# Grouped attention: one head's eight matmuls between the context products, statistics by tile, ScalarE's weights in two pieces

## The reference, cut to what matters

```python
q  = _ln(_fp8_linear_pertensor(ln_out, wq, ...))        # 8 groups x 2 heads of 128
k  = _ln(_fp8_linear_pertensor(ln_out, wk, ...))        # 8 groups x 128
v  = _fp8_linear_pertensor(ln_out, wv, ...)
core = _gqa(q, k, v)
qx = _ln(_fp8_linear_pertensor(ln_out, wqx, ...))       # 8 groups x 2 heads of 128
kx, vx = jnp.split(jnp.einsum('bsi,oi->bso', cond, w_kv_x), 2, axis=-1)
kx = _ln(kx)
xout = _gqa(qx, kx, vx)
catq = _div_clamp_fp8(jnp.concatenate([core, xout], -1), proj_smooth)
return jnp.einsum('bsi,oi->bso', catq, wproj) * (proj_in_scale * proj_w_scale)
```

## Time and profile before

| | |
|---|---|
| median of three runs | 2054.92 us (2054.7 to 2056.19) |
| the profiled execution's own time | 2054.24 us |
| its span, first to last instruction | 2052.5 us |
| mean granted TensorE clock | 0.993 |
| PE busy | 1987.3 us (97%) |
| PEld (weight loads) busy | 1568.8 us (76%) |
| DVE busy | 1406.6 us (69%) |
| ACT busy | 1229.2 us (60%) |
| POOL busy | 687.7 us (34%) |

### The profile page before, as it was taken

One profiled execution on the slowest core, in us unless ns is written; L12 is line 12 of the kernel. 1 busy time (PEld: TensorE's weight loads), 2 busy tenths in 40 slices (PEclk: granted clock), 3 DMA queues, 4 the chain that ended last, 5 costly groups with the idle time before them and its releaser, 6 DMA issues. The chain is left out here.

```text
span 2052.5 us, 31495 instructions
## 1 busy us (share of the span) xinstructions
PE 1987.3 (97%) x11048; PEld 1568.8 (76%) x11068; DVE 1406.6 (69%) x3154; ACT 1229.2 (60%) x3187; POOL 687.7 (34%) x689
## 2 busy tenths in 40 slices
PE   8999999999999999999998999999999999998998
PEld 5644789888988888898876886665766785666997
DVE  2397677777777776767567847676677658995555
ACT  2073687878887888788773445553544446772332
POOL 1300354454445454545330002324351102332442
PEclk9999999999999999999999999999999999999999
DMA  4033434232424242332323204313232220003200
GB/s 187 10 122 124 136 89 148 85 137 88 150 87 137 83 148 89 131 90 87 109 81 107 73 3 158 128 70 128 109 116 107 82 87 22 2 2 138 94 1 32
DMA packets 60173, 193.66 MB, mean 94 GB/s; under 512 B 9408, under 2 KB 28640, under 8 KB 56048
## 3 DMA queue, kind: packets, MB, share of 16 engines
q1 hardware_dynamic: 48496, 172.15, 24.5%
q10 hardware_dynamic: 9504, 8.50, 1.4%
q0 software_dynamic: 2016, 11.01, 1.3%
HBM read 171.75 MB, written 19.48 MB: 93 GB/s over the span
## 5 line engine op out<-in xcount | busy, mean ns | idle before, releaser
L988 PE MATMUL psum<-la_w_both,context 128*128 128x256 f32 (+1 forms) x1536 | 343.7, 380 | 0.0
L988 PEld LDWEIGHTS psum<-la_w_both,context 128*128 128x128 f32 (+1 forms) x1536 | 277.6, 184 | 44.9
L1465 POOL TENSOR_TENSOR norm_std<-room 128x400 f32<-128x400 f32 x75 | 70.4, 938 | 271.6 <-DVE room L1230 271.5
L944 PE MATMUL psum<-qa_xqf,qa_two 128*128 128x400 f32 x640 | 156.2, 372 | 2.3 <-PEq L60 2.3
L944 PEld LDWEIGHTS psum<-qa_xqf,qa_two 128*128 128x128 f32 x640 | 115.4, 191 | 7.5 <-issue 3.2
L3021 ACT ACTIVATE it_prob<-psum,it_nm 100x257 f32<-100x257 f32 (+1 forms) x256 | 101.7, 415 | 30.1 <-DVE it_nm L3048 29.3
L1458 POOL TENSOR_TENSOR room<-room,qa_inv 128x500 f32<-128x500 f32 x64 | 89.7, 1401 | 52.8 <-DMA qa_inv<-qa_std_rows 50.6
L1006 PE MATMUL psum<-qa_kxT,room 128*100 128x361 f32 x256 | 99.8, 471 | 3.9 <-ACT qa_kxT L1148 2.8
L1154 ACT ACTIVATE qa_prob<-psum,qa_nm 100x361 f32<-100x361 f32 x128 | 72.0, 562 | 47.3 <-DVE qa_nm L1319 46.7
L1154 ACT ACT_TABLE_LOAD x64 | 82.1, 1283 | 24.0 <-ACT qa_size L1172 18.2
L2574 POOL TENSOR_TENSOR gf_last_diff<-la_gf_what,la_gf_w 128x512 bf16<-128x512 bf16 x24 | 27.0, 1145 | 206.4 <-issue 170.2
(11 more groups left out here) (399 smaller groups left out, 5289.2 us busy)
## 6 DMA issues: line engine op xcount, KB each, us to landing
context<-in_context SPq DMA_DIRECT2D x70, 722.0 KB, 4.7
qa_inv<-qa_std_rows SPq DMA_DIRECT2D x64, 250.0 KB
qa_w_raw<-in_qa_w SPq DMA_DIRECT2D x8, 1536.0 KB, 16.1
la_gf_raw<-in_gf_w SPq DMA_DIRECT2D x16, 768.0 KB, 4.8
qa_piece<-in_tf_pieces ACTq DMA_DIRECT2D x64, 128.0 KB, 2.1
la_w_qt<-in_qa_o SPq DMA_DIRECT2D x8, 1024.0 KB, 6.1
gf_ternary<-la_gf_made POOLq DMA_DIRECT2D x7, 768.0 KB
gf_ternary<-keep POOLq DMA_DIRECT2D x7, 768.0 KB
```

What stands on the lines that cost most here:

```text
L944: mm = pe.matmul(psum[:, bank, 0:HALF], two[:, part, j, k, :], xqf[:, PART_XQ[j], k, (h % 2) * HALF:(h % 2 + 1) * HALF], start=(k == 0 and ...
L988: mm = pe.matmul(psum[0:rows, i // 2, (i % 2) * 256:(i % 2) * 256 + 256], ctxT[:, n % 2, k, t0:t0 + rows], kv_raw[:, s, k, :], start=(k == ...
```

## The change

Five things change, all inside `grouped_attention`.

1. The unit behind is no longer laid in two halves around the transposes of the probabilities. Its eight matmuls come one by one from a generator, one after each context chunk. The context product asks for one after each of its 12 chunks and there are eight, so four lie in the first tile, four in the second, and none in the third. This holds from step 6 on (`OUT_LAG`); in the steps before, the unit keeps its two halves as before.
2. `ctx_mm` counts 3 a step, one for each tile. VectorE takes the statistics of the first two tiles when the second is done, and those of the third when it is done.
3. VectorE's `normalise_keys(n)` comes ahead of `probs_out(n-1)`.
4. ScalarE's scaling of the weights (`scale_weights`) moves ahead of the exponentials; the writing of the high part stays behind them. An activation with Exp draws that table's load ahead of the scaling.
5. ScalarE takes the context values of the first two tiles from PSUM before it waits for the statistics, not after.

```diff
-                    sp.wait_ge(S_["ctx_mm"], n + 1)
+                    sp.wait_ge(S_["ctx_mm"], 3 * n + 3)
                     sp.dma_start(ctxT[:, n % 2], a["context"][(n + 2) % B]).then_inc(ctx_in[n % 2], 16)
...
-            def project_unit(u, chunks=range(C)):
+            def unit_products(u, chunks=range(C)):
                 h, j = half_and_part(u)
                 bank = bank_of(u)
...
                         mm = pe.matmul(psum[:, bank, 0:HALF], two[:, part, j, k, :],
                                        xqf[:, PART_XQ[j], k, (h % 2) * HALF:(h % 2 + 1) * HALF],
                                        start=(k == 0 and part == 0), stop=(k == C - 1 and part == 1))
-                if chunks[-1] == C - 1:
-                    mm.then_inc(S_["unit_mm"], 1)
+                        if k == C - 1 and part == 1:
+                            mm.then_inc(S_["unit_mm"], 1)
+                        yield
+
+            def project_unit(u, chunks=range(C)):
+                for _ in unit_products(u, chunks):
+                    pass
...
-            def project_context(g, s, b, n):
+            def project_context(g, s, b, n, beside):
...
                         mm = pe.matmul(psum[0:rows, i // 2, (i % 2) * 256:(i % 2) * 256 + 256],
                                        ctxT[:, n % 2, k, t0:t0 + rows], kv_raw[:, s, k, :],
                                        start=(k == 0), stop=(k == C - 1))
-                mm.then_inc(S_["ctx_mm"], 1)
+                        if k < C - 1:
+                            next(beside, None)
+                    mm.then_inc(S_["ctx_mm"], 1)
+                    next(beside, None)
...
-                project_context(g, s, b, n)
-                around = n
-                for u in behind(n):
-                    project_unit(u, range(C // 2) if around else range(C))
+                beside = unit_products(behind(n)[0]) if not early(n, OUT_LAG) and behind(n) else iter(())
+                project_context(g, s, b, n, beside)
+                if early(n, OUT_LAG):
+                    for u in behind(n):
+                        project_unit(u, range(C // 2) if n else range(C))
                 if not early(n, 1):
                     turn_probs(n - 1)
-                for u in behind(n) if around else ():
-                    project_unit(u, range(C // 2, C))
-                if not early(n, OUT_LAG):
+                if early(n, OUT_LAG):
+                    for u in behind(n) if n else ():
+                        project_unit(u, range(C // 2, C))
+                else:
                     project_out(*out_chunk(g, b, n))
...
                 measure(g, s, b, n)
+                if not early(n, 1):
+                    act.activation(spare[:, 1:2], core.eps[1.0], ACT.Exp)
+                scale_weights(n)
                 for u in ahead(n):
                     high_squares(u)
                 if not early(n, 1):
                     exps(n - 1)
                 high_weights(n)
                 if not early(n, 1):
-                    act.activation(spare[:, :], core.eps[1.0], ACT.Sqrt)
+                    act.activation(spare[:, 0:1], core.eps[1.0], ACT.Sqrt)
+                act.wait_ge(S_["ctx_st"], 3 * n + 2)
+                act.activation(vx[:, b % 2, 0:2, :], psum[:, 0, :].rearrange("p (i o) -> p i o", i=2)[:, :, P:2 * P],
+                               ACT.Copy)
                 act.wait_ge(S_["stats_ready"], n + 1)
                 act.activation(sd[:, :], mv[:, :, 1], ACT.Sqrt, bias=core.eps[1e-5]).then_inc(S_["sd_ready"], 1)
-                act.activation(vx[:, b % 2, 0:2, :], psum[:, 0, :].rearrange("p (i o) -> p i o", i=2)[:, :, P:2 * P],
-                               ACT.Copy)
                 act.activation(vx[0:R2, b % 2, 2, :], psum[0:R2, 1, P:2 * P], ACT.Copy)
...
             def context_stats(n):
-                dve.wait_ge(S_["ctx_mm"], n + 1)
                 for i, (_, rows) in enumerate(TILES):
+                    dve.wait_ge(S_["ctx_mm"], 3 * n + max(i, 1) + 1)
                     dve.bn_stats(st[0:rows, i, :], psum[0:rows, i // 2, (i % 2) * 256:(i % 2) * 256 + P]).then_inc(
                         S_["ctx_st"], 1)
...
                 context_stats(n)
+                normalise_keys(n)
                 if not early(n, 1):
                     probs_out(n - 1)
-                normalise_keys(n)
```

More of the change, by code:

```diff
@@ L798, in grouped_attention @@
         st, mv, sd, nmr = sb("st", [P, 3, 6]), sb("mv", [P, 3, 2]), sb("sd", [P, 3]), sb("nmr", [P, 3])
-        out_scale, spare = sb("out_scale", [P, 1]), sb("spare", [P, 1])
+        out_scale, spare = sb("out_scale", [P, 1]), sb("spare", [P, 2])
         nm, sums, rsum = sb("nm", [T, 4]), sb("sums", [T, 4]), sb("rsum", [T, 4])
@@ L890, in load @@
                 if g + 1 < G:
-                    sp.wait_ge(S_["ctx_mm"], max(1, g * B))
+                    sp.wait_ge(S_["ctx_mm"], 3 * max(1, g * B))
                     sp.dma_start(kv_raw[:, 1 - slot], a["qa_kv"][g + 1]).then_inc(S_["kv_in"], 16)
@@ L1119, in heads_out, with scale_weights @@
                 last.then_inc(S_["heads_ready"], 1)
-            def high_weights(n):
+            def scale_weights(n):
                 made = part_made(n, 1)
@@ L1131, in high_weights @@
                     last.then_inc(S_["v_scaled"], 1)
-                    act.wait_ge(S_["v_scaled"], g)
-                    act.activation(v3[:, g % 2, 0], w_raw[:, :, V_COL:V_COL + P], ACT.Copy).then_inc(S_["v_hi"], 1)
                     return
@@ L1140, in high_weights @@
                 last.then_inc(S_["w_scaled"], 1)
+            def high_weights(n):
+                made = part_made(n, 1)
+                if not made:
+                    return
+                g, j = made
+                if j == PARTS:
+                    act.wait_ge(S_["v_scaled"], g)
+                    act.activation(v3[:, g % 2, 0], w_raw[:, :, V_COL:V_COL + P], ACT.Copy).then_inc(S_["v_hi"], 1)
+                    return
+                u, own = (g - 1) * PARTS + j, slice(PART_COL[j], PART_COL[j] + P)
                 act.wait_ge(S_["w_scaled"], u + 1)
@@ L1219, in _ @@
                 nrm.root(act, 0, i)
-            act.activation(spare[:, :], core.eps[1.0], ACT.Gelu)
+            act.activation(spare[:, 0:1], core.eps[1.0], ACT.Gelu)
         @block.vector
```

## The result

The changed kernel takes 2081.72 us (median of four runs, 2079.31 to 2084.18) against 2055.49 (four runs of before, 2054.7 to 2056.19): a ratio of 1.0128, 95% interval 1.011 to 1.0145. It is slower, by 26.2 us. The profiled executions agree: the span went from 2052.5 to 2078.9 us, +26.4.

The account below looks back on a forecast made before the run. TensorE was taken as the bound, busy 700.74 of 701 us, so every new wait counts in full. 15.1 + 15.1 + 3.4 - 1.8 - 2.2 = +29.6 us gave 2084 us, own range 2074 to 2092, overall 2064 to 2098.

Parts of the forecast that it names:

- its own case: Whole kernel: the summed terms hold, +29.6 us, 2084 us, range 2074 to 2092; chance 0.61.
- 1 the alternation itself: TensorE, unit matmuls among context passes: taken as 0, bounds 5.9 us gained to 5 us lost.
- Part 3: Unit's first matmul waits for VectorE's low weights where n % 8 = 6: 2.16 us standstill, 7 times, 15.1 us.
- Part 2: Chains from the last context pass E: variance 0.34 us late at 39 boundaries, weighing 0.13 at 14; 15.1 us.
- Part 4: Clock falls to half after the pauses of about 2 us: 2 of 7, 3.4 us, bounds 0 and 11.9.
- Part 5: ScalarE's scaling before exponentials: their 0.5 us lateness is covered, cost 0; late variance where n % 8 = 6 goes, -1.8 us.
- 6 steps 59 to 62: End of the stage: shorter chain to the scores, E+4.64 instead of E+5.18; four boundaries by 0.54, -2.2 us.
- the case without cover: ScalarE's exponentials late with nothing covering them: 0.5 x 35 = 18 us.
- second reading: TensorE: alternation hides the weight load, 0.014 us off each of 424 matmuls, -5.9 us; rival total 2045, chance 0.05.

Follow-up runs that it names:

- low part early: Changed kernel, but where n % 8 = 6 VectorE makes the weights' low part ahead of the score maxima: 2062.7 us, ratio to before 1.0031.
- short square: Changed kernel with the low part made before the maxima where n % 8 = 6, and GpSimd squaring only half of each unit's columns: 2059.26 us, one run.
- edit 1 alone: Kernel before with only the unit's matmuls one by one between the context products, none of the other four edits: 2109.94 us, ratio 1.0263.
- two halves: Changed kernel with the unit's eight matmuls back in two halves around the probabilities' transposes, other edits kept: 2050.27 us, ratio to before 0.9971.
- probabilities first: Changed kernel with the low part made before the maxima where n % 8 = 6, and VectorE's probabilities again ahead of the keys: 2066.92 us, ratio 1.0051.
- eighth experiment: Changed kernel, low part before maxima (n % 8 = 6), probabilities before keys, GpSimd squaring and subtracting half the columns, ScalarE scaling one of three head tiles: 2043.81 us, one run.

## Why the prediction was right

It gave 2084 with 2074 to 2092 for its own case; 2081.7 was measured. By its own terms, against the profiled execution:

```
term                                      predicted   measured
1 the alternation itself                       0         0       0.614 a period against 0.614
2 late chains, boundaries to 7 to 59       +15.1     +14.8      (low part early: 13.1 + 7 x 0.25)
3 standstill at the weights                +15.1     +14.8      7 x 2.12
4 the clock                                 +3.4      +3.3      2 falls of 1.66
5 late variance, n % 8 = 6                  -1.8      -1.8
6 steps 59 to 62                            -2.2      -1.5
  steps 0 to 5                               0        -1.5
  outside the steps                          0        -1.5
```

**Part 3** was right in place, count and size: 2.16 forecast, 2.12 found, and removed by moving one instruction. Reading the code for which step makes a part and which step uses it gave it; nothing in the profile of before points to it, because there the part was ready at 732.58 and the unit started at 735.15, 2.6 us later.

**Part 2** was right in sum and partly right in kind. It put the squares last, 0.34 late, and the weighing at 0.13. The weighing was worth 0.21 to 0.24, which is what steps after an "ahead" unit lost and what the short square left, and the squares only what came on top: 0.28 us less on GpSimd brought 0.05. The start was near (0.16 late against 0.13), but the sum passed that lateness on as it was, and it grew to 0.23 by the key transposes. So the sum came out right partly by luck: 39 boundaries lost 0.29 instead of 0.34, and 14 lost 0.22 instead of 0.13. The other forecast times were near: variance E+4.67 against 4.63 (the hand-over on GpSimd took 0.08, 727.67 to 727.75, and not 0.14), copy of the keys E+4.97 against 4.89, root E+0.71 against 0.72. Three chains that end within 0.1 us of one another can't be ranked by such a sum, and it does not matter for the total, but it does for the mending: shortening one of them alone gained almost nothing, or moved the wait.

**Part 4** was a draw from few cases, and luck. Of the five pauses between 1.76 and 1.99 us in the trace of before three were followed by a fall, which would have given four of seven; I took two. Two is what the profiled execution had; the run with edit 1 alone had three falls behind the same pauses. The four runs of the changed kernel span 4.9 us, about three falls, and the slowest had the lowest granted clock (0.989 against 0.991 and 0.992). Not all of them need be these: behind step 62, where nothing was changed but the end of the stage, the profiled executions of the eleven kernels had three to seven falls.

**Part 5** held in the changed kernel: the transposes never waited. The run with two halves shows the cover was needed: with the unit behind the context product again, the early scaling costs 0.35 us in the steps with n % 8 = 3. It is 6 x 0.35 = 2.1 us there, and not the 0.5 x 35 = 18 us that I had put on the case without cover: in the other steps the late exponentials were still in time.

**Left out or too small.** I set steps 2 to 5 at zero, and they gave 1.9 us back, step 0 another 0.4, as the unit keeps its old place there and only the shorter chain shows. Step 1 took 0.8 us more (16.94 against 16.13): TensorE stands there for 2.93 us instead of 1.88, and both kernels have a fall of the clock there. This step is between 14.6 and 17.0 us in the eleven kernels, and no run isolates why.

In steps 59 to 62 I expected 0.54 a boundary and found 0.15, 0.30, 0.30 and 0.77 (the last in step 62, where in the kernel before the transposes of the probabilities start at E+0.63 and in the changed one at E-0.16). The chain ends at the copy of the keys at E+4.77, not 4.54. TensorE, held at the weighing, hands over the transposed keys later. TensorE and ScalarE in step 61 of the changed kernel, where E is 1075.01:

```profile
1078.62 0.48 PE L1006 MATMUL psum<-ident,qa_nrm_x 128*128 128x128 f32 x3
1079.13 0.65 ACT L1169 ACTIVATE qa_kxT<-psum,params 128x361 f32<-128x361 f32 x1 [0.21 <-PE psum L1006]
```

ScalarE stands idle for 0.21 us until the transposes are done. With the probabilities first the weighing is on time, the transposes start at E+3.38 instead of 3.61, and the copy ends at E+4.70 although the normalised keys come later. So the term took the squares out of the ScalarE chain and forgot the chain over TensorE beside it.

The 1.5 us outside the steps stay unexplained. Over the eleven kernels the time before step 0 is 206.7 to 207.8 us and that from step 63 on 984.8 to 989.1, so differences of this size say nothing about the change.

## What to carry to other kernels

Moving an engine's filler from behind a producer to ahead of it changes no work on that engine and shortens the cover of every chain that starts at the producer: list them all with their ends, since they may be tied, and then shorten or re-cover them together, or move only as much as the slack allows (four matmuls instead of eight). For each instruction that now runs earlier, look at every semaphore it waits for and ask in which step, and behind what, that count is reached; a slack of a whole phase can become a standstill in one step of eight. When an edit comes with others meant to support it, run them without it: here they alone were the gain.

## What the runs showed of the hardware that I had not expected

- A fp32r matmul of 400 columns keeps its 0.183 us between float32 passes, and a float32 pass of 256 columns its 0.217; putting them in turn changes neither. The second reading of the Trainium skill's spacing rule (TensorE: Matmul & The Clock Gate, "Back-to-back issue gap"), by which a neighbour hides the weight load and the spacing falls towards the estimated 169 ns, is not borne out. The median period of two passes and one matmul is 0.614 us in the changed kernel and 0.615 in the eighth experiment (408 periods), where 0.014 less would be 0.600; and steps 6 to 58 take 723.8 us there against 723.9 with two halves.
- Nearly equal pauses (1.80 to 1.87 us of recorded idle time) had unequal ends: behind two of seven in one execution, and three of seven in another, 3.4 us were granted half the clock, and behind the others none. What separates them these runs don't show.
- TensorE started again within 0.05 us of VectorE's last write (748.26 to 748.31).
